# Cross-attention tail: alternating score banks for the last two units, and a bank for each of the last five outputs

## The reference

```
q = heads(x @ to_q_w)
h_g = softmax(q @ heads(ctx_g @ to_k_g)^T / sqrt(32)) @ heads(ctx_g @ to_v_g)   for g in txt, obj, oth, ip
out = merge(h_txt + h_obj + h_oth + h_ip) @ to_out_w + to_out_b + x
```

## Time and profile before

| what | value |
|---|---|
| median of 3 runs | 2551.22 us |
| the profiled execution | 2547.66 us |
| its span, first to last instruction | 2545.6 us |
| TensorE busy (matmul) | 2488.2 us, 98% |
| ScalarE busy | 1709.0 us, 67% |
| VectorE busy | 1598.5 us, 63% |
| mean granted TensorE clock | 0.987 |

### The profile page before, as it was taken

How to read it: one execution, slowest core, us unless ns; L and a number is a source line. 1 busy time by engine, 2 the same in 40 slices (tenths; PEclk the granted TensorE clock), 3 DMA queues, 4 the chain that set the end, 5 groups by cost and what they waited for, 6 DMA issues and landing times.

```text
span 2545.6 us, 37372 instructions
## 1 busy us (share of the span) xinstructions
PE 2488.2 (98%) x13125; PEld 1841.4 (72%) x13125; DVE 1598.5 (63%) x2963; ACT 1709.0 (67%) x3829; POOL 408.3 (16%) x565
## 2 busy tenths in 40 slices
PE   7999999999999997999999999999999999999997
PEld 7999999999999984456666666666666666666654
DVE  4131111211111246899999999999999999999981
ACT  3132212212121236999999999999999999999992
POOL 0000000000000002322232232232232232232210
PEclk9999999999999996999999999999999999999999
DMA  9473333323234255567677677676676666666641
GB/s 236 129 242 129 118 110 111 123 98 131 100 128 147 97 125 122 96 147 148 125 152 145 125 155 143 124 157 141 127 155 143 127 150 141 134 149 139 136 102 57
DMA packets 287619, 341.25 MB, mean 134 GB/s; under 512 B 89407, under 2 KB 181695, under 8 KB 287431
## 3 DMA queue, kind: packets, MB, share of 16 engines
q1 hardware_dynamic: 234032, 275.93, 48.6%
q10 hardware_dynamic: 53398, 62.93, 7.7%
HBM read 186.71 MB, written 83.89 MB: 106 GB/s over the span
## 4 chain that ended last, share of the span: by engine, by line
PE 58%; ACT 3%; issue 1%; DVE 0%; DMA 0%; SPq 0%; DVEq 0%
PE s_ps L392 13%; PE st_ps L408 12%; PE om_ps L422 12%; PE om_ps L463 11%; PE om_ps L440 10%; ACT probs L509 1%; ACT s_ps L517 1%; ACT small L525 0%; DMA out<-in_xT 0%; DVE out L648 0%; DVE sums L596 0%; DVE heads L641 0%; DVE heads L636 0%; DVE sums L597 0%; SPq L285 0%
## 5 line engine op out<-in xcount | busy, mean ns | idle before, releaser
L517 ACT ACTIVATE s_ps<-s_ps,negmax 128x427 f32<-128x427 f32 x1280 | 762.1, 601 | 10.5 <-DVE small L582 8.9
L573 DVE TENSOR_REDUCE negmax<-s_ps 128x2 f32<-128x854 f32 x640 | 667.0, 1042 | 95.1 <-PE s_ps L392 86.2
L509 ACT ACTIVATE probs<-st_ps 128x1024 f32<-128x1024 f32 x640 | 662.7, 1036 | 58.9 <-PE st_ps L408 55.1
L1203 PE MATMUL s_ps<-w_split,ctx_split 128*128 128x320 f32 (+2 forms) x3072 | 453.7, 309 | 0.8 <-DVE w_split L1099 0.8
L1203 PEld LDWEIGHTS s_ps<-w_split,ctx_split 128*128 128x128 f32 (+2 forms) x3072 | 451.3, 186 | 2.0 <-DVE w_split L1099 1.1
L392 PE MATMUL s_ps<-kpack,qpack 96*128 96x512 f32 x1280 | 436.5, 423 | 14.5 <-ACT s_ps L517 14.5
L1183 PE MATMUL st_ps<-ctx_split,w_split 128*128 128x428 f32 (+2 forms) x2280 | 431.6, 349 | 6.7 <-DVE ctx_split L1099 4.6
L408 PE MATMUL st_ps<-qpack,kpack 104*128 104x512 f32 x1280 | 419.2, 409 | 18.7 <-ACT probs L509 13.0
L1183 PEld LDWEIGHTS st_ps<-ctx_split,w_split 128*128 128x128 f32 x2280 | 411.5, 190 | 23.0 <-DVE ctx_split L1099 4.9
L392 PEld LDWEIGHTS s_ps<-kpack,qpack 96*128 96x128 f32 x1280 | 216.5, 192 | 265.9 <-ACT s_ps L517 223.8
L358 POOL TENSOR_TENSOR small<-small,negmax 128x616 f32<-128x616 f32 x160 | 196.2, 1226 | 1109.7 <-DVE negmax L590 1109.7
(11 more groups left out here) (56 smaller groups left out, 1430.9 us busy)
## 6 DMA issues: line engine op xcount, KB each, us to landing
qpack<-q_out SPq DMA_DIRECT2D x240, 256.0 KB, 5.9
kpack<-kT SPq DMA_DIRECT2D x240, 256.0 KB, 5.1
kT<-k_out ACTq DMA_DIRECT2D x160, 217.5 KB, 2.3
ctx_split_raw<-in_ctxT SPq DMA_DIRECT2D x128, 214.0 KB, 4.5
xs_raw<-in_xT SPq DMA_DIRECT2D x80, 256.0 KB, 5.2
out<-in_xT SPq DMA_DIRECT2D x80, 256.0 KB, 5.9
out_yT<-out SPq DMA_DIRECT2D x80, 256.0 KB, 3.4
v_ip_rows<-v_out ACTq DMA_DIRECT2D x48, 320.0 KB
```

Of the source, the lines that this page charges most:

```text
L509: nc.scalar.activation(probs[:, at:at + 2, :], st_ps[:, :, :], ACT.Exp).then_inc(p_done, 1)
L517: last = nc.scalar.activation(s_ps[:, n % 2, z, SMALL:TOK], s_ps[:, n % 2, z, SMALL:TOK], ACT.Exp, bias=negmax[:, r, IP, j, t:t + 1], accu ...
L573: nc.vector.tensor_reduce(negmax[:, r, IP, j, t0:t0 + 2], s_ps[:, n % 2, :, SMALL:TOK], AX_X, ALU.max, negate=True).then_inc(s_max, 1)
L1203: last = nc.tensor.matmul(v_ps[0:rows, v0 % 2, half, 0:CH // 2], c[run % 2][:, px, q, a:a + rows], w[W[name][0]][:, pw, q, half * (CH // 2 ...
```

## The change

The transposed scores of units 78 and 79 (`LATE`) alternate between `st_ps` and the first two of the four `s_ps` banks, and each duo but duo 0 waits for the exponential of the duo before the last. Duo 1 of unit 78 also waits until the last row-score exponential has read `s_ps`. In slots 82 and 83 the 15 products of outputs 73 and 74 are spread, two to a step; their `add_output` moves from step 3 to step 7 of the slot. Outputs 75 to 79 (`LAST` on) each have a bank: 75 to 78 the four `s_ps` banks, 79 `m_ps`. The 12 products of each that read heads of units 75 to 78 are issued before the last heads exist: those of output 75 ahead of the last `values(79, 3)`, those of 76 to 79 behind it. The last three products of each come after all of them. The five last residuals are loaded in one go in slot 80, ahead of that slot's `pack_queries(79)` on SyncE, into the buffer `x_raw`, once the last query product is done.

```diff
+LAST = UNITS - QC
+LATE = UNITS - 2
+Y_LATE = {k: (2 * k, min(2 * k + 2, PRODUCTS)) for k in range(STEPS)}
...
+    def transposed(u, duo):
+
+        return s_ps[:, 0, :, :] if u >= LATE and duo % 2 else st_ps[:, :, :]
+
+    def product_bank(w):
+
+        return m_ps if w in (LAST - 1, UNITS - 1) or w < LAST else s_ps[:, 1 - (w - LAST) // 2, (w - LAST) % 2, :]
+
+    def output_rows(w):
+
+        return out[:, w % OR, :] if w < LAST else x_raw[:, w - LAST, :]
...
+        def load_last_residuals():
+
+            sp.wait_ge(q_acc, UNITS)
+            for w in range(LAST, UNITS):
+                b, rows = block_rows(w)
+                sp.dma_start(output_rows(w), d["xT"][b, rows, :]).then_inc(res_last[w - LAST], 16)
...
-            if unit(m - Y_LAG):
+            if unit(m - Y_LAG) and m - Y_LAG < LAST:
                 load_residual(m - Y_LAG)
+            if m == UNITS:
+                load_last_residuals()
...
-            if n > 0:
+            if u >= LATE and duo > 0:
+                pe.wait_ge(p_done, n - 1)
+            elif n > 0:
                 pe.wait_ge(p_done, n)
+            if u == LATE and duo == 1:
+                pe.wait_ge(s_exp, PAIRS * UNITS)
...
+        def output_upto_last(w):
+
+            pe.wait_ge(o_lo, UNITS - 1)
+            if w in (LAST + 2, LAST + 3):
+                pe.wait_ge(p_done, DUOS * UNITS)
+            if w == UNITS - 1:
+                pe.wait_ge(y_added, LAST)
+            for n in range(PRODUCTS - len(PASSES)):
+                z, (pw, po) = n // len(PASSES), PASSES[n % len(PASSES)]
+                nc.tensor.matmul(product_bank(w), wo[:, pw, z, (w - LAST) * P:(w - LAST + 1) * P],
+                                 heads[:, (LAST + z) % HR, po, :], start=(n == 0), stop=False)
+
+        def output_last(w):
+
+            pe.wait_ge(o_lo, UNITS)
+            for n, (pw, po) in enumerate(PASSES):
+                last = nc.tensor.matmul(product_bank(w), wo[:, pw, QC - 1, (w - LAST) * P:(w - LAST + 1) * P],
+                                        heads[:, (UNITS - 1) % HR, po, :], start=False, stop=(n == len(PASSES) - 1))
+            last.then_inc(y_done, 1)
...
+        def late_slot(m):
+
+            for k in range(STEPS):
+                u, duo = duo_at(m, k)
+                if unit(u):
+                    scores_t(u, duo)
+                if k == STEPS - 2 and m - 4 == UNITS - 1:
+                    output(m - Y_LAG, range(*Y_LATE[k]))
+                    output(m - Y_LAG, range(*Y_LATE[k + 1]))
+                    output_upto_last(LAST)
+                if k % 2 == 0:
+                    values(m - 4, k // 2)
+                if k < STEPS - 2 or m - 4 < UNITS - 1:
+                    output(m - Y_LAG, range(*Y_LATE[k]))
+
...
-            for m in range(FIRST, UNITS + Y_LAG):
+            for m in range(FIRST, LATE + 4):
                 slot(m)
+            for m in range(LATE + 4, UNITS + 4):
+                late_slot(m)
+            for w in range(LAST + 1, UNITS):
+                output_upto_last(w)
+            for w in range(LAST, UNITS):
+                output_last(w)
...
-                if k == 3 and unit(m - Y_LAG):
+                if k == (3 if m < LATE + 4 else STEPS - 1) and unit(m - Y_LAG):
                     add_output(m - Y_LAG)
```

More of the change, by code:

```diff
@@ L188, in attention @@
     res_in = [sem(f"res_in{r}") for r in range(OR)]
+    res_last = [sem(f"res_last{c}") for c in range(QC)]
+    y_last = sem("y_last")
     y_out = [sem(f"y_out{r}") for r in range(OR)]
@@ L284, in store_output @@
             sp.wait_ge(y_added, w + 1)
-            sp.dma_start(d["yT"][b, rows, :], out[:, w % OR, :]).then_inc(y_out[w % OR], 16)
+            sp.dma_start(d["yT"][b, rows, :], output_rows(w)).then_inc(y_out[w % OR] if w < LAST else y_last, 16)
+        def load_last_residuals():
[3 more added lines that the diff above has]
+                sp.dma_start(output_rows(w), d["xT"][b, rows, :]).then_inc(res_last[w - LAST], 16)
         def first_keys():
@@ L330, in rest @@
             for r in range(OR):
-                sp.wait_ge(y_out[r], 16 * len(range(r, UNITS, OR)))
+                sp.wait_ge(y_out[r], 16 * len(range(r, LAST, OR)))
+            sp.wait_ge(y_last, 16 * QC)
         return SyncOps(load_rows, pack_queries, first_keys, first_values, rest)
@@ L402, in scores_t @@
                     pe.wait_ge(rows_set, QKR)
-            if n > 0:
+            if u >= LATE and duo > 0:
+                pe.wait_ge(p_done, n - 1)
+            elif n > 0:
                 pe.wait_ge(p_done, n)
+            if u == LATE and duo == 1:
+                pe.wait_ge(s_exp, PAIRS * UNITS)
             for z in range(2):
                 kt, j = (2 * duo + z) // HPU, (2 * duo + z) % HPU
-                last = nc.tensor.matmul(st_ps[:, z, :], kpack[r][0:ROWS_ST, j, kt * P:(kt + 1) * P],
+                last = nc.tensor.matmul(transposed(u, duo)[:, z, :], kpack[r][0:ROWS_ST, j, kt * P:(kt + 1) * P],
                                         qpack[r][0:ROWS_ST, j, :], start=True, stop=True)
@@ L508, in prob @@
             at = (ITEMS * u + x) % PR
-            nc.scalar.activation(probs[:, at:at + 2, :], st_ps[:, :, :], ACT.Exp).then_inc(p_done, 1)
+            nc.scalar.activation(probs[:, at:at + 2, :], transposed(u, duo), ACT.Exp).then_inc(p_done, 1)
         def ip_sums(u, p):
@@ L645, in add_output @@
             dve.wait_ge(y_done, w + 1)
-            dve.wait_ge(res_in[w % OR], 16 * use(w, OR))
-            nc.vector.scalar_tensor_tensor(out=out[:, w % OR, :], in0=m_ps[:, :],
-                                           scalar=bias[:, w % QC:w % QC + 1], in1=out[:, w % OR, :],
+            if w < LAST:
+                dve.wait_ge(res_in[w % OR], 16 * use(w, OR))
+            else:
+                dve.wait_ge(res_last[w - LAST], 16)
+            nc.vector.scalar_tensor_tensor(out=output_rows(w), in0=product_bank(w),
+                                           scalar=bias[:, w % QC:w % QC + 1], in1=output_rows(w),
                                            op0=ALU.add, op1=ALU.add).then_inc(y_added, 1)
```

## The result

The changed kernel took 2532.37 us (median of 7 runs, 2524.51 to 2535.46). The kernel before, in 7 runs that include the three shown above, took 2547.55 (2537.67 to 2551.96). The medians are 15.2 us apart; the estimate of their ratio is 0.9948, with a 95% interval of 0.993 to 0.9966: 13.2 us less (8.7 to 17.8), on a forecast of 12.9. The forecast time of 2538.3 us and its range, 2535.5 to 2542.0, missed all the same, because they stood on a median of 2551.22.

What follows compares the result with a forecast made beforehand. No engine is full, so a chain of latencies bounds the kernel's last 65 us. Gains of 3.2 and 9.8 us make 13.0, less 0.1 for stores: 2551.2 - 12.9 = 2538.3 us, range 2535.5 to 2542.0.

Steps and rivals of the forecast that it cites:

- The profile against the median: Level of the whole kernel: the profiled execution's 3.56 us gap was put on the median, 2551.2, giving 2538.3 us.
- the loop: Transposed scores, duo (78, 0) to (79, 7): 3.20 us per two duos instead of 3.70 plus lumps; 3.2 us gained.
- the end: After duo (79, 7): TensorE has no wait left up to the last products; 9.8 of the 13.0 us gained.
- The 6.43 against 3.68 us: Output 75's 15 products took 6.43 us before, later rounds 3.68; the excess was not to come again.
- The moved add: On VectorE, add_output(73) ahead of heads(78) makes values(79, 0) start late: 1.38 us lost, TensorE idle about 1.9.
- The bridge: Duo (79, 7) to the last store's issue, summed from its parts: 31.16 us before, 21.4 now.
- Residual loads: Five loads ahead of pack_queries(79) in SyncE's queue: taken as nothing, bounds 0 and 4.4 us.
- second rival: The loads ahead of pack_queries(79) delay unit 79's queries or unit 77's log-sums: 0 to 4.4 us, middle 2540.5; chance 0.12.
- First rival: The clock falls at the wait for heads(78), costing 2.75 us: 2541.0; chance 0.17.
- fourth rival: After the idle at 2499 the clock stays at the lower level to the kernel's finish: 2565 us; chance 0.02.
- third rival: Alternating banks for transposed scores brings nothing: period stays 1.85 us per duo, 3.2 not gained, 2542.9; chance 0.09.

## Why the prediction was right and where it was wrong

- **The step that failed** is "The profile against the median. [...] I put the difference on the median: 2551.2 - 12.9 = 2538.3 us". The difference held; the level didn't. The profiled execution shown stood 3.6 us under the median of three, and I took both for something that stays. The runs showed a spread from 2533 to 2552 us for one and the same kernel, mostly from how long TensorE sits at its lower level at the end of the projection part, and medians of 2540 to 2548. The range was built from the costs of the edit alone, 6.5 us wide, narrower than the spread of the kernel it started from. From the median of seven, 2547.55, the same difference gives 2534.7, 2.3 us from the measured 2532.37; the 18.9 us between 2551.22 and 2532.37 are 13.2 of the edit and the rest the starting point. Some 3 us of the first session are not explained by the clock.
- **The 12.9 against 13.2** is in part luck. In the two profiles that the table compares, the loop missed by -0.7 and the end by +0.5, and the low clock took 1.2 us ahead of duo (78, 0). The 6.43 against 3.68 us went into the end's gain as if certain, and the repeated profile of the kernel before does not have it there. That profile lost as much elsewhere (5.1 us of low clock from duo (78, 0) on in both; 1.7, 3.4 and 1.7 in the changed kernel's three): against it the end gained 7.3 us and the loop 4.8. The total held, 60.58 and 61.32 against 48.47, 49.48 and 48.42.
- **The loop.** Forecast 3.2 us gained from (78, 0) to (79, 7), measured 2.5. The period was 3.32 and not 3.20: I took 0.47 for two products behind a values group, which cost 0.57 there (0.66 as the chain counts them): the first of their weight loads begins only when that group is through, together with the product. Four periods and the turn to unit 79 make the 0.7. The timeline of the changed kernel has that weight load, after 0.84 us without one:

```profile
2490.84 0.30 PEld L494 LDWEIGHTS om_ps<-heads,wo 128*128 128x128 f32 x2 [0.84 <-issue]
```

- **The moved add.** Forecast 1.38, measured 1.34 in the trace and 1.24 by taking it away (47.08 less 45.84).
- **The end.** Forecast 9.8 gained, measured 10.3. TensorE's part was right; I had VectorE set the pace of the last adds at 0.78, from the length of their records, but from start to start they cost no more than TensorE's 0.68. The bridge's terms for the kernel before add up to 31.4 and not 31.16; nothing rests on that. The clock's part of the 10.3 is the chance told above.
- **Residual loads.** Taken as nothing, with bounds 0 and 4.4: up to duo (77, 0) nothing to 0.4 in five profiles of six, 2.5 in the sixth, and 4.0 by duo (78, 0) there. The mechanism of the second rival is shown (landing 7.3 to 9.2 us instead of 4.3 to 7.3), and the sign set for it, a wait of scores(79, 0) for a DMA, came in three profiles of six. The landings agree with what the Trainium skill (DMA: Bandwidth & Descriptors, "Queues, rings and completion order") says, that each DMA engine takes the descriptors of a ring in order. Its usual price was hidden by ScalarE, which holds the scores back anyway.
- **The clock.** First rival: right in kind, 1.3 us instead of 2.75. The low clock lasted half as long (3.4 us against 6.8), and TensorE had waits to give up in that loop. From duo (79, 7) to the last product the clock stayed up in all ten profiles that have the new end, the one without early products too; in the kernel before it fell there in one of two. The fourth rival did not occur.
- **The alternation brings nothing** (third rival): refuted by the kernel with one bank pair.

## What to carry to other kernels

When an edit is worth 0.5%, forecast the difference and take the level, and the width of the range, from how the unchanged kernel scatters; three runs do not show that. Measure such an edit on a stretch of the trace between two fixed instructions, in more than one profile of both kernels: for the changed kernel 20.04 us came out three times while whole runs scattered by 10, but for the kernel before the same stretch read 30.38 and 27.31. And when work is spread to fill waits, look at what is queued behind its last consumer: here an add of 0.75 us held up two others by 1.3.

## What the runs showed of the hardware

The granted clock fell at different places in different profiles of the same code: at the wait for heads(78), 1.7 us without a matmul, it fell in two of five profiles and held in three; behind the wait of 1.54 us for the heads of unit 79 in the kernel before it was low in one profile and up in the other (6.43 and 3.70 us for the same 15 products). After a fall the low level lasted from 3 to 10 us at a time near the end of the kernel. In the last 150 us of the projection part it came to 31 to 55 us in all (15.3 to 27.4 us lost, at half the clock). That made up most of the scatter between runs of the three later sessions: less the clock's term the deviation is 1.7 us and not 3.9. And five loads of 262 kB put ahead of a packing DMA raised its median landing from 5.7 to 7.9 us though they had been issued in 2.25 us, 0.45 each and not the 0.76 of the earlier trace rows.
